# Attention and mixture-of-experts block on one core: the rows of negated maxima sent at steps 22 and 6 of a turn instead of 24 and 9

## The reference

```python
q = proj(layernorm(x), Wq, bq); k = proj(ctx, Wk, bk); v = proj(ctx, Wv, bv)     # 8 heads of 16
scores = einsum('bhqd,bhkd->bhqk', q, k) / sqrt(16)
attn = softmax(scores, axis=-1)
x = x + tanh(g_xattn) * einsum('bhqk,bhkd->bhqd', attn, v)
h = rmsnorm(layernorm(x)) * w
probs = softmax(h @ router_w); topv, topi = top_k(probs, 2)                      # 8 experts
moe = sum over the 2 chosen: topv/sum(topv) * (silu(h@gate) * (h@up)) @ down
x = x + tanh(g_ffn) * (moe + shared expert)
```

## Time and profile before

| | |
|---|---|
| median of 3 runs | 1496.56 us (1496.29 to 1497.58) |
| the profiled execution | 1503.05 us |
| its span, first to last instruction | 1501.2 us |
| PE busy | 1404.3 us, 94% |
| DVE busy | 999.0 us, 67% |
| ACT busy | 875.5 us, 58% |
| POOL busy | 861.9 us, 57% |
| DMA from `m_rows`, share of the chain that ended last | 8% |
| the same, issue to landing | 1.7 us at least, 3.8 us median, 8.9 us at most |
| idle PE before line 1291, all of the span | 27.3 us, of it 21.8 us until a DMA from `m_rows` |

### The profile page before, as it was taken

One profiled execution on the slowest core, in us unless ns is written; L12 is line 12 of the kernel. 1 busy time (PEld: TensorE's weight loads), 2 busy tenths in 40 slices (PEclk: granted clock), 3 DMA queues, 4 the chain that ended last, 5 costly groups with the idle time before them and its releaser, 6 DMA issues.

```text
span 1501.2 us, 25163 instructions
## 1 busy us (share of the span) xinstructions
PE 1404.3 (94%) x7290; PEld 727.9 (48%) x7290; DVE 999.0 (67%) x2172; ACT 875.5 (58%) x1720; POOL 861.9 (57%) x1276
## 2 busy tenths in 40 slices
PE   5889999999999989999999999998899899999997
PEld 1223333333333333333333333277688787778886
DVE  5768888888888877888888888655654232323332
ACT  2467777777777767777777776734234333333332
POOL 6437667667677766777676763632212445555554
PEclk9899999999999999999999999999999999999999
DMA  5857677677767767776776765265453867775664
GB/s 141 194 136 202 179 194 197 177 196 190 170 175 186 192 168 173 179 195 177 192 188 167 181 168 129 89 211 134 113 198 86 240 146 157 187 185 111 113 113 78
DMA packets 183329, 247.93 MB, mean 165 GB/s; under 512 B 31045, under 2 KB 105420, under 8 KB 183198
## 3 DMA queue, kind: packets, MB, share of 16 engines
q1 hardware_dynamic: 160846, 208.42, 52.7%
q0 software_dynamic: 18256, 37.38, 13.1%
q10 hardware_dynamic: 4096, 0.53, 0.2%
HBM read 141.85 MB, written 103.88 MB: 164 GB/s over the span
## 4 chain that ended last, share of the span: by engine, by line
PE 52%; DMA 18%; issue 14%; POOL 5%; DVE 4%; ACT 3%; SPq 1%; POOLq 1%; ACTq 1%; another core or an unknown queue 0%; DVEq 0%
PE bank L1363 13%; PE bank L1320 11%; PE bank L1291 10%; PE bank L1269 9%; DMA arena<-m_rows 8%; DMA pv_d<-arena 4%; DMA out<-xs,ids 3%; POOL xs L743 3%; PE bank L1254 2%; PE bank L1307 2%; PE bank L1296 2%; ACT arena L1111 1%; DVE row_max L851 1%; PE bank L1258 1%; DMA arena<-pv_d 1%
## 5 line engine op out<-in xcount | busy, mean ns | idle before, releaser
L851 DVE TENSOR_REDUCE row_max<-bank 128x1 f32<-128x512 f32 x1024 | 674.9, 683 | 123.4 <-PE bank L1269 106.0
L1111 ACT ACTIVATE arena<-bank 128x512 f32<-128x512 f32 x1024 | 572.0, 608 | 247.5 <-PE bank L1291 224.3
L1291 PE MATMUL bank<-arena 98*128 98x512 bf16 x1024 | 391.8, 385 | 27.3 <-DMA arena<-m_rows 21.8
L1269 PE MATMUL bank<-arena 96*128 96x512 bf16 x1024 | 397.2, 390 | 18.6 <-DVE row_max L851 11.0
L1320 PE MATMUL bank<-arena 128*32 128x512 f32 x2048 | 275.9, 611 | 1.4 <-ACT arena L1111 1.1
L755 POOL DMA_INDIRECT out<-xs,ids x71 | 112.5, 1584 | 194.3 <-ACT xs L1195 148.9
L1291 PEld LDWEIGHTS bank<-arena 98*128 98x128 bf16 x1024 | 103.0, 101 | 202.4 <-ACT arena L1111 74.6
L1269 PEld LDWEIGHTS bank<-arena 96*128 96x128 bf16 x1024 | 101.1, 99 | 174.7 <-DVE row_max L851 90.7
L1363 PE MATMUL bank<-w_ring,h_hi 128*128 x568 | 184.1, 405 | 0.0
L1184 ACT ACTIVATE arena<-bank 128x256 f32<-128x256 f32 x103 | 39.5, 384 | 198.1 <-PE bank L1363 188.4
L644 POOL TENSOR_TENSOR arena<-arena 128x512 bf16<-128x512 f32 x62 | 71.5, 1152 | 138.6 <-ACT arena L1103 135.9
(11 more groups left out here) (174 smaller groups left out, 2002.2 us busy)
## 6 DMA issues: line engine op xcount, KB each, us to landing
arena<-parts_q SPq DMA_DIRECT2D x64, 256.0 KB
pv_d<-arena SPq DMA_DIRECT2D x32, 512.0 KB, 7.0
w_ring<-split_d SPq DMA_DIRECT2D x60, 256.0 KB
parts_k<-arena SPq DMA_DIRECT2D x96, 128.0 KB
arena<-parts_k SPq DMA_DIRECT2D x32, 384.0 KB
parts_q<-arena SPq DMA_DIRECT2D x96, 128.0 KB
arena<-in_w SPq DMA_DIRECT2D x36, 256.0 KB, 5.5
arena<-in_ctx SPq DMA_DIRECT2D x32, 256.0 KB, 3.1
```

Source lines behind the costliest of these rows:

```text
L851: nc.vector.reduce_max(row_max[b % 2][:, u:u + 1], m_ps[(STEPS * b + u) % M_BANKS][:], AX_X).then_inc(s_mx, 1)
L1111: nc.scalar.activation(probs[group % 3][:, j, :], e_ps[n % E_BANKS][:], ACT.Exp, scale=float(DH) ** -0.5).then_inc(s_exp, 1)
L1269: nc.tensor.matmul(m_ps[n % M_BANKS][:], q_stack[b % 3][0:STACK, h, qt * P:(qt + 1) * P], k_stack[b % 3][0:STACK, h, :], start=True, stop= ...
L1291: nc.tensor.matmul(e_ps[n % E_BANKS][:], k_stack[b % 3][0:SHIFTED, h, kt * P:(kt + 1) * P], q_stack[b % 3][0:SHIFTED, h, :], start=True, s ...
```

## The change

Two numbers of a table of steps. The scalar engine issues the DMAs of half 0 behind its exponential of step 22 and not 24, and those of half 1 behind that of step 6 and not 9.

```diff
-ROW_AT = (24, 9)
+ROW_AT = (22, 6)
```

## The result

| | before | changed |
|---|---|---|
| median of 4 runs each | 1496.42 us (1492.91 to 1497.58) | 1481.02 us (1477.49 to 1483.93) |
| ratio, 95% interval | | 0.9879 (0.9845 to 0.9912) |
| the profiled execution, its span | 1503.05, 1501.2 us | 1483.93, 1482.1 us |
| PE, DVE, ACT, POOL busy | 1404.3, 999.0, 875.5, 861.9 us | 1401.0, 998.2, 865.9, 862.2 us |
| chain that ended last, DMA from `m_rows` | 8% | 2% |

The change makes the kernel 1.2% faster: 15.4 us between the medians, 18 us by the ratio. By the ratio the 1496.56 us become 1478.4 us. The forecast was 1486.5 us and its range began at 1480.0 us: the sign was right, and the gain was forecast too small.

The account below looks back on a forecast made before the run. Bound by matrix-unit waits for half 0's rows before step 0. Waits 7.8 us plus clock 6.5 us made 14.3 us on the profiled execution, cut to 10 for unprofiled runs: 1496.5 to 1486.5 us, range 1480.0 to 1495.0 us.

Parts of the forecast that it names:

- What bounds the kernel: Before step 0 of turns, the matrix unit waits for half 0's rows of negated maxima, 22.6 us in 19 waits.
- the freed place at step 24: Scalar queue at step 24, freed of 1.1 us of issue: following work 0.1 to 0.2 us earlier at most, counted nothing.
- The cover at step 22: Scalar engine before step 23's activation: 1.24 us of idle time covers the short wait and 1.1 us of issue.
- The landing: Half 0's row DMAs: issued 2.0 us earlier, landing taken as the full 2.0 us earlier, range 0 to 2.0.
- the slow half of a transfer: Half 0's DMA packets: 32 of 64 ran 2 us later, read as one half standing behind the sync queue's transfers.
- Rival A: Sync queue's backlog sets half 0's landing: in full 1496.5 us, chance 0.09; in part, 1 us earlier, 1490.5 us, 0.10.
- The price of the waits: Waits before step 0: first 0.9 us of each is free, so eleven longer ones are worth 7.8 us.
- Waits under 4 us: Sign in the profile after: the matrix unit's waits for the rows under 4 us in sum.
- The clock: Matrix unit behind the longest waits: granted clock drops to 1.2 GHz, costing 6.5 us that go with the waits.
- the discount from 14.3 to 10 us: Unprofiled runs thought to lose less: middle of 7.8 and 14.3 is 11, less 1 us for rows still late.
- Rival B: Unprofiled runs have hardly any waits over 0.9 us, so only one or two shorten: 1494.5 us, chance 0.07.
- rival C: Scalar engine's issue pair gets long, 3.5 us, among the sync queue's issues; slower, 1510 us, chance 0.06.

Follow-up runs that it names:

- the other chip: Changed kernel again (steps 22 and 6) against the kernel before, on another chip: 1498.30 us against 1526.22 us, ratio 0.9818.

## Why the prediction was right and wrong

**What bounds the kernel: right.** The waits before step 0 were the loss; they fell from 23.2 to 6.3 us, and with half 0 alone the gain is complete within the intervals (0.9895). That half 1 and the freed place at step 24 are worth nothing held too (1.0010 for half 1).

**The cover at step 22: right, and it mattered more than I wrote.** "This covers both the short wait and the issue" is what the timeline after shows, the same 1.24 us of idle time. What an uncovered issue costs was put as a remark; one step later it turned a change of no effect into one 1.2% slower.

**The landing: right in size, by luck in part.** "I take the full 2.0 us" came out as 1.95 us (1.3 us with half 0 alone, for the same issue). But the forecast let the landing follow the issue, and between 4.33 and 5.65 us it does not: an issue 0.4 us earlier or 0.9 us later than before moves it by 0.13 us at most, one 3.8 us later by 0.64 us. Between 2.79 and 4.33 us it moves by 1.8 us, and why is only known in part. The store of the tokens, which the text had named, is worth 1.04 us when it is moved by itself. The load of the values I had not named: the first of the two DMAs is issued ahead of it in 17 of 26 turns, but both only in four. The turns of the changed kernel in which the second DMA overtook nothing landed as early as the others. Three readings were wrong beside this. The packets that ran 2 us later were not the slow half of a transfer but the second DMA. The k writes were not overtaken by the change: the rows were ahead of them before, by 2.4 us. And SP's two issues at 450.26 and 450.93 us, the loads of lines 474 and 475, just ahead of the 451.1 us at which the rows were to be issued, stand in the same stretch of the trace and were left out. Rival A in full was wrong; in part, a landing 1 us earlier, it has the store's share.

**The price of the waits: the sum was right, its terms were not.** 14.3 us were forecast on the profiled execution; its attention part lost 13.8 us. The terms can be checked roughly, by an estimate. The closing steps give 25 x 0.73 = 18.3 us. The lower level shrank from 13.7 to 3.4 us, and 10.3 us less at half the clock give back 5.2 us at most, not 6.5 us. The 25 turns became 14.5 us shorter, so 18.3 + 5.2 - 14.5 = 9.0 us were paid back inside them; the forecast, which freed 0.9 us in each of eleven waits and the 4.9 us of short ones, had 14.8 us paid back, of 22.6 us of waits. A wait was worth more than forecast, and fewer waits went: that the two errors and the clock's cancel is luck. "Waits under 4 us" was too hopeful: 7.5 us over the span, two of them over 2 us. Turns came to 28.45 us on average, not 28.0 to 28.3.

**The clock: right in kind.** Stretches at the lower level went with the waits, but not all: one of 3.4 us behind a wait of 2.42 us is left, where none was forecast.

**The step that failed: the discount from 14.3 to 10 us.** "The unprofiled runs have fewer of these losses" was inferred from one number, that the median lay 6.5 us below the profiled execution. They have the losses in full: the runs gave 15.4 us by the medians and 18 us by the ratio, the edit of half 0 alone 1501.76 x 0.0105 = 15.8 us, and the other chip 28 us. The clock says so too: in the 23 executions of the kernel before that stand beside half 0 alone, its mean over the execution was between 0.975 and 0.985, 0.979 at the median, where the profiled execution of the earlier trace rows had 0.981. So they do not have less of the lower clock. The 6.5 us were scatter: those 23 executions lie between 1495.81 and 1511.51 us, and a profiled execution lies now above its median (by 2.9 us in the changed kernel), now below (by 5.3 us with half 0 alone, by 7.0 us with the maxima turned at step 17). Without the discount of 4.3 us the forecast would have been 1482.2 us, against 1481.0 us by the medians and 1478.4 us by the ratio. Rival B, a stronger form of the same inference, was wrong for the same reason, and rival C did not come: pairs of issues at half 0 took at most 1.49 us in the changed kernel.

## What to carry to other kernels

When a small transfer is late, do not expect its landing to follow its issue. Here issues 1.3 us apart landed together, and what a move gives had to be measured at several steps. Look at which transfers of the other queues it would overtake, turn by turn, since one turn can be a favourable one. A DMA issued by a compute engine needs an idle stretch to lie in: here 1.1 us of issue without one made the kernel 1.2% slower. And a profiled execution a few microseconds above the median is no reason to discount the losses that its trace shows.

## What the runs showed of the hardware

- Two DMAs of 4 KB took 7.3 us from the first issue to the last landing at the median (half 0 of the kernel before, 4.77 to 12.03), against 1.7 us for the quickest single one. The same landing for issues 1.3 us apart (steps 23 to 26) means that there an earlier issue only waits longer.
- A pause of PE of 2.42 us was followed by the lower clock and one of 2.62 us was not. Nor does it take such a wait: on the other chip, with the maxima turned at step 17 and the moments moved, the lower clock came eight times between 140 and 930 us, 30.7 us in all, with 0.2 us of waits before step 0 there. The length of the pause before a turn does not tell the outcome alone.
- The kernel before took 1496.42, 1501.76, 1498.96 and 1526.22 us as a median in four sessions, and the same change gave 1.2% and 1.8%. The intervals of the two ratios overlap a little, so a different gain on different chips is likely and not shown; ratios are to be taken on one chip only.
- Removing every wait before step 0 between 140 and 930 us (maxima turned at step 17) did not give a clearly faster kernel, 0.4% on its chip. That the last microseconds of waiting are free because the vector engine is near enough behind would explain it; no run shows it.
